# Transformer block in fp32: projections spread over attention's slots, values mixed beforehand per half of the queries

## Reference

```
xn = layernorm(x)
q, k, v = xn @ Wq, xn @ Wk, xn @ Wv      # 32 query heads, 8 key/value heads, head size 64
q, k = rope(q, k)
scores = q k^T / 8                        # allowed: j <= i and i - j < 128
attn_out = softmax(scores) v @ Wo
h = fwht(xn * SU_ug) / 64
g = silu(h @ W_gate^T * scale) * (h @ W_up^T * scale)
ffn_out = fwht(g * SU_dp) / 64 @ W_down^T * scale
out = x + attn_out + ffn_out
```

## Time and profile before

| | |
|---|---|
| median of 3 runs | 1442.33 us (1441.26 to 1446.47) |
| profiled execution | 1443.7 us, of which the span of its instructions is 1441.2 us |
| granted TensorE clock, mean | 0.993 |
| busy | PE 93%, PE's weight loads 73%, DVE 63%, ACT 52%, POOL 48% |
| DMA | 138.35 MB, mean 96 GB/s |

### The profile page before, as it was taken

The page is one execution under the profiler, slowest core; times in us unless marked ns, Lnnn a source line. Parts: engine busy times, 40 slices in busy tenths (PEclk is TensorE's granted clock), DMA queues, the critical chain, the costliest instruction groups (busy, mean ns, idle before and its releaser), DMA issues.

```text
span 1441.2 us, 34032 instructions
## 1 busy us (share of the span) xinstructions
PE 1335.5 (93%) x12776; PEld 1046.0 (73%) x12776; DVE 913.0 (63%) x1496; ACT 745.3 (52%) x2685; POOL 686.0 (48%) x719
## 2 busy tenths in 40 slices
PE   6798889989999999999989999998999999999998
PEld 3576667867777677777768777786777777777776
DVE  5656665467745677457764677556774567745775
ACT  2345564266633667146652666426663366724665
POOL 5225543266542665236542555425653266523664
PEclk9899999999999999999999999999999999999999
DMA  6223441424222342323414144042432234231331
GB/s 228 66 81 104 118 125 60 139 62 127 83 89 84 87 126 69 113 66 108 120 53 132 43 119 120 30 147 60 123 85 90 87 82 119 82 109 51 90 106 58
DMA packets 71554, 138.35 MB, mean 96 GB/s; under 512 B 15328, under 2 KB 29152, under 8 KB 71136
## 3 DMA queue, kind: packets, MB, share of 16 engines
q1 hardware_dynamic: 70400, 135.46, 32.7%
q10 hardware_dynamic: 992, 0.73, 0.2%
HBM read 73.21 MB, written 12.58 MB: 60 GB/s over the span
## 4 chain that ended last, share of the span: by engine, by line
PE 64%; DVE 14%; POOL 8%; issue 5%; ACT 4%; SPq 2%; DMA 1%; POOLq 0%; DVEq 0%
PE PROJ L897 14%; PE PROJ L899 13%; PE PROJ L898 13%; PE O L1071 7%; PE TR L1052 6%; POOL e_sb L490 6%; PE S L1041 5%; DVE negmax L830 3%; DVE S L828 3%; ACT e_sb L597 2%; PE S L897 2%; DVE acc L741 2%; PE S L898 2%; PE S L899 2%; DVE S L823 2%
## 5 line engine op out<-in xcount | busy, mean ns | idle before, releaser
L490 POOL TENSOR_TENSOR e_sb<-e_sb,rinv 128x512 f32<-128x512 f32 x256 | 266.2, 1040 | 354.6 <-DVE rinv L835 349.9
L597 ACT ACTIVATE e_sb<-S,negmax 128x128 f32<-128x128 f32 x1024 | 362.1, 369 | 110.3 <-DVE negmax L830 109.0
L714 DVE TENSOR_TENSOR prod<-PROJ,rope_sb 128x1024 f32<-128x1024 f32 x160 | 195.4, 1222 | 117.5 <-PE PROJ L899 116.8
L823 DVE COPY_PREDICATED S<-diagonal_key,S 128x512 f32<-128x512 int8 x192 | 133.2, 694 | 178.5 <-PE S L1041 178.3
L607 ACT ACTIVATE pt_sb<-TR 128x512 f32<-128x512 f32 x256 | 153.2, 598 | 178.8 <-PE TR L1052 176.9
L1041 PEld LDWEIGHTS S<-k_stack,q_stack 64*64 64x64 f32 x5632 | 169.6, 133 | 79.6 <-issue 53.5
L1052 PE MATMUL TR<-ident,e_sb 128*128 128x128 f32 x1024 | 168.0, 287 | 62.4 <-POOL e_sb L490 58.7
L1041 PE MATMUL S<-k_stack,q_stack 64*64 64x64 f32 (+2 forms) x5632 | 211.1, 274 | 7.8 <-ACT e_sb L597 7.8
L597 ACT ACTIVATION_READ_ACCUMULATOR e_sb<-S,negmax 128x1 f32 x1024 | 212.2, 207 | 0.0
L830 DVE TENSOR_REDUCE negmax<-S 128x4 f32<-128x512 f32 x256 | 177.0, 691 | 8.8
L1052 PEld LDWEIGHTS TR<-ident,e_sb 128*128 128x128 f32 x1024 | 108.0, 141 | 95.3 <-POOL e_sb L490 77.5
(11 more groups left out here) (96 smaller groups left out, 2589.4 us busy)
## 6 DMA issues: line engine op xcount, KB each, us to landing
q_stack<-qy SPq DMA_DIRECT2D x512, 64.0 KB, 2.0
wq_ring<-wq_split_d SPq DMA_DIRECT2D x56, 512.0 KB, 3.5
wo_ring<-wo_split_d SPq DMA_DIRECT2D x56, 512.0 KB, 3.9
k_stack<-ky SPq DMA_DIRECT2D x256, 64.0 KB, 2.0
x_in<-x SPq DMA_DIRECT2D x8, 512.0 KB, 4.6
wq_split_d<-wq_ring SPq DMA_DIRECT2D x8, 512.0 KB, 2.8
wo_split_d<-wo_ring SPq DMA_DIRECT2D x8, 512.0 KB, 4.0
out<-acc SPq DMA_DIRECT2D x8, 512.0 KB, 4.9
```

The lines of the kernel that those rows point to most:

```text
L490: nc.gpsimd.tensor_tensor(e, e, r, ALU.mult).then_inc(norm_done, 1)
L597: last = nc.scalar.activation(e_sb[:, n % 2, r, :], s_heads(n, 1)[:, r, :], ACT.Exp, bias=negmax[:, n % 2, r:r + 1], accum_out=rowsum[:, n ...
L714: nc.vector.tensor_tensor(prod[:, 2 * part:2 * part + 2, :], both, rope_sb[:, :, :], ALU.mult).then_inc(prod_done, 1)
L823: nc.vector.copy_predicated(own.rearrange("p r (a k) -> p r a k", a=2), diagonal_key[:, :, :].rearrange("p r (a k) -> p r a k", a=2), diagonal
```

## The change

Four things are changed. First, the query projections of heads 2 and 3 leave the FFN and become fillers of slots 0, 1, 4 and 5; all parts of query and key projections are now in even slots from 6 on. Second, in odd slots the transposes stand behind the fillers. Third, the values of a pair of steps are computed for each half of the 128 queries (64 columns a head). For the first half the base is the block before, as ever; for the second half it is `v_mix`, whose first 64 keys are of the own block and whose last 64 are of the block before. Only the two 64x64 diagonal blocks of weights then need the correction with `v_step`, each in its own quarter of the array (64 keys, 64 outputs). Block 0 of a head needs no mask and no correction. Half 0 of O lies in O's bank, half 1 in the first two heads of TR, the bank of the transposes. So O is copied and split in two instructions, the transposes of odd slots wait for `o_split`, and `o_low` stands at the head of VectorE's odd slot. Fourth, smaller things: fold_weights goes over column blocks first, so that the first gate matmuls wait for a part of the folded weights only; xn and silu have buffers of their own; the DMA queue's order and the slots in which row 0's weights are split follow the new table.

```diff
-    ROPE_SLOTS = {("q", 4, 0): (3, 5), ("k", 1, 0): (7, 9), ("q", 5, 0): (11, 13),
-                  ("q", 6, 0): (15, 17), ("q", 7, 0): (19, 21), ("k", 0, NEXT): (29, 31)}
-    NORM_SLOT = 24
-
-    WQ_SPLIT_IN_FFN = {1: 2, 2: 3, 3: 4}
-    WQ_SPLIT_SLOT = {4: 5, 11: 6, 17: 7}
+    ROPE_SLOTS = {("q", 2, 0): (0, 1), ("q", 3, 0): (4, 5), ("q", 4, 0): (6, 8), ("k", 1, 0): (10, 12),
+                  ("q", 5, 0): (14, 16), ("q", 6, 0): (18, 20), ("q", 7, 0): (22, 24), ("k", 0, NEXT): (28, 30),
+                  ("q", 0, NEXT): (32, 34)}
+    NORM_SLOT = 25
+
+    WQ_SPLIT_IN_FFN = {1: 2, 3: 3}
+    WQ_SPLIT_SLOT = {4: 4, 9: 5, 12: 6, 20: 7}
...
+        O_half = [O[:, 0:2 * P].rearrange("p (s m q) -> p s m q", s=2, m=2),
+                  TR[:, 0:2, :].rearrange("p s (m q) -> p s m q", m=2)]
...
+                for n in range(LAST_SLOT + 1):
                     if 1 <= n <= STEPS:
                         normalise(n - 1)
-                    if n >= 2:
+                    if 2 <= n <= STEPS + 1 and (n - 2) % TT:
                         mask(n - 2)
...
                 def o_copy(pair):
                     i = 2 * pair % TT
                     act.wait_ge(pv_done, b * STEPS + 2 * pair + 2)
-                    nc.scalar.activation(o_p[0][:, :, i * P:(i + 2) * P],
-                                         O[:, :].rearrange("p (m q) -> p m q", m=2), ACT.Copy
-                                         ).then_inc(o_copied, 1)
+                    for a in range(2):
+                        last = nc.scalar.activation(o_half(0, i, a), O_half[a].rearrange("p s m q -> p m s q"), ACT.Copy)
+                    last.then_inc(o_copied, 1)
...
                 dve.wait_ge(o_copied, (row * STEPS) // 2 + pair + 1)
-                low(o_p[1][:, :, i * P:(i + 2) * P], O[:, :].rearrange("p (m q) -> p m q", m=2),
-                    o_p[0][:, :, i * P:(i + 2) * P]).then_inc(o_split, 1)
+                for a in range(2):
+                    last = low(o_half(1, i, a), O_half[a].rearrange("p s m q -> p m s q"), o_half(0, i, a))
+                last.then_inc(o_split, 1)
...
+                def value_mix(i):
+
+                    dve.wait_ge(v_done, b * TT + i + 1)
+                    HP = P // 2
+                    nc.vector.tensor_copy(v_mix[0:HP, i - 1, :], v_sb[0:HP, i, :])
+                    nc.vector.tensor_copy(v_mix[HP:P, i - 1, :], v_sb[HP:P, i - 1, :]).then_inc(v_mixed, 1)
+
                 for n in range(LAST_SLOT + 1):
+                    if n >= 5 and n % 2:
+                        o_low(b, (n - 5) // 2)
                     if n < STEPS:
                         fold(n)
                     if 1 <= n <= STEPS:
                         inverse_sum(n - 1)
-                    if n >= 5 and n % 2:
-                        o_low(b, (n - 5) // 2)
+                    if n in (0, 3, 4):
+                        value_mix(max(n - 1, 1))
...
                     pe.wait_ge(norm_done, b * STEPS + n + 1)
                     if n >= 1:
                         pe.wait_ge(t_copied, b * STEPS + n)
+                    if n >= 3 and n % 2:
+
+                        pe.wait_ge(o_split, (b * STEPS + n - 3) // 2 + 1)
...
+                def values_mixed(pair):
+
+                    HP = P // 2
+                    pe.wait_ge(t_copied, b * STEPS + min(2 * pair + 3, STEPS))
+                    pe.wait_ge(v_done, b * TT + min(2 * pair + 2, TT))
+                    pe.wait_ge(v_mixed, b * (TT - 1) + min(2 * pair + 1, TT - 1))
+                    if pair:
+                        pe.wait_ge(o_split, b * STEPS // 2 + pair)
+                    for s in range(2):
+                        g, i = divmod(2 * pair + s, TT)
+                        heads = slice(g * D, (g + 1) * D)
+                        for a in range(2):
+                            v = v_mix[:, i - 1, heads] if i and a else v_sb[:, max(i - 1, 0), heads]
+                            for odd in range(2):
+                                last = nc.tensor.matmul(O_half[a][odd * D:(odd + 1) * D, s, :, :], v,
+                                                        pt_sb[:, (2 * pair + s) % 4, odd:REP:2, a * HP:(a + 1) * HP],
+                                                        start=s == 0, stop=False)
+                    pe.wait_ge(v_stepped, b * (TT - 1) + min(2 * pair + 1, TT - 1))
+                    for s in range(2):
+                        g, i = divmod(2 * pair + s, TT)
+                        heads = slice(g * D, (g + 1) * D)
+                        if i:
+                            pe.wait_ge(p_masked, b * MASKS + masks_upto(2 * pair + s))
+                            for odd in range(2):
+                                for a in range(2):
+                                    half = slice(a * HP, (a + 1) * HP)
+                                    last = nc.tensor.matmul(O_half[a][odd * D:(odd + 1) * D, s, :, :],
+                                                            v_step[half, i - 1, heads], p_cur[half, (2 * pair + s) % 4, odd:REP:2, half],
+                                                            start=False, stop=s == 1)
+                    last.then_inc(pv_done, 2)
...
                 for n in range(LAST_SLOT + 1):
                     if n < STEPS:
                         scores(n)
-                    if 2 <= n <= STEPS + 1:
+                    if 2 <= n <= STEPS + 1 and n % 2 == 0:
                         transposes(n - 2)
                     for kind, row, m, part in fillers(b, n):
...
+                    if 2 <= n <= STEPS + 1 and n % 2:
+                        transposes(n - 2)
                     if n >= 4 and n % 2 == 0:
-                        values_mixed(n - 4)
-                        values_mixed(n - 3)
+                        values_mixed((n - 4) // 2)
```

More of the change, by code:

```diff
@@ L107, in attention_and_ffn_block @@
             for j in HIDDEN_AFTER[n]:
-                if n and j == HIDDEN_AFTER[n][0]:
+                if n == 1 and j == HIDDEN_AFTER[n][0]:
                     USES += [("q", b, n, 0), ("gate", b, j, 0), ("q", b, n, 1), ("up", b, j, 0)]
@@ L392, in _ @@
                 stack_k(1)
-                for m in (2, 3):
-                    if not b:
-                        save_wq(m)
-                    load_wq(b, m + 2)
                 if not b:
-                    save_wq(4)
+                    save_wq(2)
+                load_wq(b, 4)
                 for n in range(2, NKV):
@@ L406, in _ @@
                         save_wo(1)
-                        save_wq(5)
-                    if not b and n == 4:
-                        save_wq(6)
-                    if not b and n == 5:
-                        save_wq(7)
-                    if 3 <= n <= 4:
-                        load_wq(b, n + 3)
-                    if 5 <= n <= 6 and b + 1 < BATCH:
-                        load_wq(b + 1, n - 5)
                     if n >= 3:
@@ L419, in _ @@
                         load_wo(b, n - 1)
+                    m = {2: 5, 3: 6, 5: 7}.get(n)
+                    if m:
+                        if not b:
+                            save_wq(m - 2)
+                        load_wq(b, m)
+                    if n >= 6:
+                        if not b:
+                            save_wq(n)
+                        if b + 1 < BATCH:
+                            load_wq(b + 1, n - 6)
                 if not b:
@@ L458, in rotate @@
                     pool.wait_ge(*stacked(row, n - 2, q_stacked, Q_STACKED))
+                elif kind == "q" and row:
+                    pool.wait_ge(*stacked(row - 1, NKV + n - 2, q_stacked, Q_STACKED))
                 if kind == "k" and (n or row):
@@ L506, in value_step @@
                                             ).then_inc(v_stepped, 1)
-                rotate(b, "q", 0)
+                if not b:
+                    rotate(b, "q", 0)
                 pool.wait_ge(x_loaded, b * 16 + 16)
@@ L512, in _ @@
                 nc.gpsimd.tensor_copy(acc[:, :, :], x_in[:, :, :]).then_inc(acc_init, 1)
[L513 to L515 removed]
+                rotate(b, "q", 1)
+                for n in range(LAST_SLOT + 1):
                     if 1 <= n <= STEPS:
                         normalise(n - 1)
[L518 removed]
+                    if 2 <= n <= STEPS + 1 and (n - 2) % TT:
                         mask(n - 2)
[L520 to L521 removed]
+                    if n in (0, 3, 4):
+                        value_step(max(n - 1, 1))
                     for kind, m, row in rope_jobs(b, n, 1):
@@ L633, in _ @@
                         h_high(j - 1)
-                    if not b:
+                    if not b and n in WQ_SPLIT_IN_FFN:
                         wq_high(WQ_SPLIT_IN_FFN[n])
@@ L975, in _ @@
             for n in range(CT * 4):
[L976 removed]
+                k, c = divmod(n, CT)
                 if n >= 4:
@@ L1005, in hidden @@
                     dst = bank(name, b, j, 0)
+                    if not b:
+                        pe.wait_ge(fold_lo, CT * (j // 2 + 1))
```

(22 more changed lines are left out.)

40 lines of the change are left out of this document (20 added, 20 removed).

## The result

The changed kernel takes 1493.14 us (1490.77 to 1495.93, 4 runs), the kernel before 1442.31: a ratio of 1.0348, 95% interval 1.0329 to 1.0366. It is slower by 51 us where 21 were forecast.

A forecast was written before the change was run, and what follows sets the result against it. The prediction took TensorE work, busy 93% of the span, as the bound. Seven rows at +14.0, row 0 at +8 and the start at -1 gave +21 us: 1465 profiled, 1463 as median, range 1434 to 1492.

The forecast's parts named there:

- The loop: Steady attention: even transposes wait behind O copy, low part, fold, reciprocal and POOL; pairs 7.54 or 7.75 us against 7.29.
- S: Zero of the loop's times: start of an odd slot, where the even slot's values ended; even transposes forecast at S + 4.33.
- forecast 130.2: Steady row's attention in us, with 14 loops of 7.65, against 122.2 before: +8.0.
- Sum 8 + 12 + 2.6 + 2.4 = 25, +6: Row 0's attention: excess over a steady row from first splits, wo pieces and wq pieces; 25 us against 18.9 before.
- The 8 us left for the first splits: Row 0's attention, slots 2 to 4: estimated share of its excess for weight splits that stay there.
- The last row: Attention of the final row, counted among seven rows at +8.0 us each.
- FFN and start: Four query projections leave each FFN, -6.0 us a row; earlier start on folded weights ahead of row 0, -1 us.
- The sum: Whole kernel: seven rows +14.0, row 0 +8, start -1, together +21 us on the profiled 1443.7.
- The shorter loop: Rival: attention loop parts at their lower bounds, loop 7.40 us, total 1435 us; chance 0.20.
- TensorE as the bound: Rival: low part of O done early enough, so pairs take only TensorE's work, total 1356 us; chance 0.10.
- Records: Rival: value base's 128-column records keep 0.107 us each, base 1.71 us, +96 us, total 1559; chance 0.08.
- Query stacks: Rival: DMAs of q5 to q7 come late, 1 us beyond slack 24 times, +24 us, total 1487; chance 0.10.

The follow-up runs named there:

- a_split_later: Changed kernel, but in row 0 VectorE takes the low part of each weight piece one slot later than ScalarE makes its high part: 1464.4 us.
- a_rinv_first: Changed kernel, but in odd slots from 5 on VectorE takes the even step's reciprocal ahead of O's low part, not behind the fold: 1425.0 us.
- mix_on_scalar: Changed kernel with reciprocal first, weights' low parts a slot later, silu's table load behind a copy, mixed value blocks made by ScalarE instead of VectorE: 1393.2 us.
- new_table_mix: Changed kernel with reciprocal first, weights' low parts a slot later, silu's table load behind a copy, first mixed value block in slot 3, not 0: 1401.5 us.

## Why the prediction was too small, step by step

- **The loop** was right as a mechanism and near in size: pairs of 7.68 and 7.88 us against 7.54 and 7.75. The transposes start at S + 4.38 instead of S + 4.33, and the values take 1.30 and 1.51 instead of 1.22 and 1.43, as the step to the corrections costs more than the 0.15 taken. The copies of O take 0.69 up to the low part (0.71 in the sum), the low parts 0.67 up to the fold (0.61). Fourteen loops of 0.13 are 1.9 us of the 2.6 by which steady attention exceeds the forecast 130.2. Over rows 1 to 6 the attention was +61.8 where 48 was forecast.
- **Row 0** is the step that failed: "Sum 8 + 12 + 2.6 + 2.4 = 25, +6". The excess was 37.7, so the term was +18.8, and with the loop row 0's attention grew by 29.4 where 14 was forecast. The delay of the fold was read well: in slots 17, 25 and 29 it starts at S + 3.86, against 4.0. What the delay costs was not. The sum took it as a delay of the even transposes alone. It left out that the odd transposes, too, now wait for what VectorE has put off (17.0 us, 8 times), and it had no term for the clock, though the 0.96 of the earlier trace rows showed one: 16.1 us here against 5.9 before. So, against row 3, slots 17 and 18 lose 2.6 us, near the 2.4 of the sum, but 25 and 26 lose 3.7, 29 and 30 4.9, and 21 and 22, with the late piece, 7.3. The sum also has five wo pieces from slot 12 on where the table has six; the sixth stands in slot 32, and from slot 31 on row 0 is 3.8 us longer than row 3. The 8 us left for the first splits were near: slots 4 to 6 lose 9.2. a_split_later shows that the lost time hangs on the one order: its row 0 exceeds row 3 by 3.8 us.
- **The last row** was taken as any other. Before, it was 4.7 us shorter than a steady one, since its last slots lack fillers (117.5 us); after, only 1.7 (131.1). A loop that waits does not get shorter when work is taken out of it. +13.6 where 8 was forecast.
- **FFN and start** were right: -6.2 for each of seven FFNs against -6.0, and -8.2 ahead of row 0's attention against -7. The first matmul of the FFN came at 35.20 instead of 42.94, and the second gate projection then waited 5.0 us for silu, as the prediction said.
- **The sum**: 15.4 from row 0, 13.8 from rows 1 to 6, 5.6 from the last row and -2.8 from the rest are the 32.0 by which +53.0 exceeds +21. So row 0, where a wait and the clock had no term, is about half of the miss; the other half is the loop and the last row, right in kind and short in size.
- **The rivals.** The shorter loop, and TensorE as the bound, are false as the changed kernel stands; yet a_rinv_first goes most of the way to the latter in steady rows, by moving one reciprocal: their idle time is 6.3 to 7.7 us instead of 15.6. Records do not set the pace: the base's groups of four start 0.22 apart, 0.055 each. The rule of the Trainium skill that was cited for that rival, page "TensorE: Matmul & The Clock Gate", section "The mechanism", by which weight loads overlap with running matmuls only where the row group differs, disagrees with these rows, and the measurement decides. Query stacks cost 1.5 us in all.

## What to carry to other kernels

When a buffer is shared to save work on the busiest engine, list every instruction that must now be done before the next writer, and look at what stands ahead of each on its own engine: here the price was not in the arithmetic but in one reciprocal behind a fold, one table load ahead of a copy, and one split that made VectorE wait. A wait of an in-order engine costs all that is queued behind it, so let the consumer of another engine's result stand a slot later than its producer. And cost a row with irregular work by itself, its clock too.

## What the runs showed of the hardware

- TensorE's extra idle time in row 0 (21.7 us, single waits up to 4.3) cost most of its length again afterwards, in slower records: 16.1 us. Not each wait did: behind one of 1.64 us the granted clock was 1.00, behind another 0.58.
- VectorE's fp32 copy of 64x512 from SBUF to SBUF does not get through beside a running POOL instruction: 0.39 to 0.42 us when none runs at its start, 1.17 as the median of the second copies in the changed kernel. There 23 copies began beside a running POOL instruction, and each ended 0.28 to 0.29 us after that instruction. ScalarE's copies of the same blocks in mix_on_scalar took 0.62 to 0.65 us with or without one. The Trainium skill, page "SBUF — State Buffer", section "SBUF: two separate sides", describes the port pair that both share as an exclusive lock for a whole instruction; the rows of new_table_mix agree.
- Matmuls of 128 columns in 128x64 tiles pass at 0.055 us each with a weight load for every one.
